# A new order of work behind the last depthwise convolution: scores, values and keys moved among TensorE, VectorE and ScalarE

## The reference, cut to what matters

```python
q, k, v = proj(Wq, bq), proj(Wk, bk), proj(Wv, bv)      # of X, per image (256, 32)
scores = jnp.einsum('bic,bjc->bij', q, k)
a = jax.nn.softmax(scores, axis=1)                      # over i
x = jnp.einsum('bij,bjc->bic', a, v)
return X + x
```

## Time and profile before

| | us |
|---|---|
| median of 3 runs | 115.43 |
| the three runs | 114.87 to 115.98 |
| the profiled execution | 114.63 |
| its span | 112.8 |

### The profile page before, as it was taken

One profiled execution on the slowest core, in us unless ns is written; L12 is line 12 of the kernel. 1 busy time (PEld: TensorE's weight loads), 2 busy tenths in 40 slices (PEclk: granted clock), 3 DMA queues, 4 the chain that ended last, 5 costly groups with the idle time before them and its releaser, 6 DMA issues.

```text
span 112.8 us, 5243 instructions
## 1 busy us (share of the span) xinstructions
PE 95.6 (85%) x2376; PEld 53.0 (47%) x2376; DVE 76.1 (67%) x154; ACT 86.7 (77%) x204; POOL 12.6 (11%) x25
## 2 busy tenths in 40 slices
PE   0193999989978999989987999989799999997660
PEld 0021477665525468324543663345454665575320
DVE  0004996534739897999578889936473889889751
ACT  4049787597998738896579899757989989879950
POOL 7010000000000000000000003893000040004200
PEclk9999589999999999999999999999999999999999
DMA  2890098870000000000000000000000100020022
GB/s 54 254 360 33 5 103 131 93 112 6 0 6 9 0 9 6 0 6 6 0 6 0 6 6 0 0 6 0 6 6 0 68 31 0 6 85 11 0 93 93
DMA packets 2261, 4.55 MB, mean 40 GB/s; under 512 B 576, under 2 KB 832, under 8 KB 2240
## 3 DMA queue, kind: packets, MB, share of 16 engines
q1 hardware_dynamic: 2096, 4.20, 16.1%
q10 hardware_dynamic: 144, 0.03, 0.2%
HBM read 1.96 MB, written 1.05 MB: 27 GB/s over the span
## 4 chain that ended last, share of the span: by engine, by line
PE 54%; ACT 19%; DVE 11%; DMA 7%; SPq 4%; issue 3%; ACTq 0%; DVEq 0%
PE ps L399 13%; ACT prob L771 7%; PE ps L482 6%; ACT hpad L722 5%; DMA x<-x_in 5%; PE ps L447 4%; PE ps L510 4%; DVE unit L936 4%; PE ps L494 3%; PE ps L475 3%; ACT prob L758 3%; DMA prob<-npad 3%; PE ps L287 3%; PE ps L383 3%; PE ps L298 2%
## 5 line engine op out<-in xcount | busy, mean ns | idle before, releaser
L399 PE MATMUL ps<-hpad,third 32*32 32x450 f32 (+2 forms) x864 | 36.5, 563 | 0.6 <-ACT hpad L722 0.4
L771 ACT ACTIVATE prob<-ps,smax 128x256 f32<-128x256 f32 x56 | 25.8, 479 | 3.7 <-DVE smax L983 3.6
L936 DVE SCALAR_TENSOR_TENSOR unit<-hpad,third,unit 128x544 f32<-128x544 f32 x32 | 23.9, 797 | 0.0
L983 DVE TENSOR_REDUCE smax<-ps 128x2 f32<-128x512 f32 x26 | 16.6, 685 | 6.5 <-PE ps L494 3.4
L399 PEld LDWEIGHTS ps<-hpad,third 32*32 32x32 f32 x864 | 14.0, 103 | 8.9 <-issue 4.2
L264 POOL TENSOR_TENSOR v_tok<-v_tok,row_inv 128x256 f32<-128x256 f32 x7 | 5.1, 740 | 88.8 <-DVE row_inv L993 88.8
L771 ACT ACTIVATION_READ_ACCUMULATOR prob<-ps,smax 128x1 f32 x56 | 11.8, 210 | 0.0
L722 ACT ACTIVATE hpad<-ps,third 128x1024 f32<-128x1024 f32 x8 | 8.7, 1115 | 2.9 <-PE ps L383 2.4
L863 DVE SCALAR_TENSOR_TENSOR npad<-x,first,rstd 128x256 f32<-128x256 f32 x8 | 3.5, 480 | 10.1 <-ACT rstd L700 10.1
L510 PE MATMUL ps<-prob,v_tok 128*32 128x256 f32 x128 | 8.1, 382 | 2.3 <-ACT prob L758 1.1
L691 ACT ACTIVATE swapped<-ps 128x512 f32<-128x512 f32 x8 | 4.5, 594 | 7.2 <-PE ps L287 7.2
(11 more groups left out here) (87 smaller groups left out, 144.7 us busy)
## 6 DMA issues: line engine op xcount, KB each, us to landing
prob<-npad SPq DMA_DIRECT2D x16, 74.4 KB, 2.9
x<-x_in SPq DMA_DIRECT2D x4, 256.0 KB, 5.6
y<-m SPq DMA_DIRECT2D x3, 256.0 KB, 2.6
third<-third_in SPq DMA_DIRECT2D x1, 456.5 KB, 6.7
second<-second_in SPq DMA_DIRECT2D x1, 401.5 KB, 5.8
y<-m SPq DMA_DIRECT2D x2, 128.0 KB, 1.9
first<-first_in ACTq DMA_DIRECT2D x1, 33.0 KB, 4.3
```

What stands on the lines that cost most here:

```text
L399: last = pe.matmul(inside(pixels(ps[quadrant(rotated(r, g)), banks[g], :]), tap), c3("taps")[quadrant(r), tap * C:(tap + 1) * C], inside(p ...
L771: last = act.activation(prob[:, G * (slot_turn(s) % PROBS) + g, jt * NPIX:(jt + 1) * NPIX], ps[:, banks[q], jt * NPIX:(jt + 1) * NPIX], AC ...
L936: dve.scalar_tensor_tensor(out=sums, in0=source, scalar=weight, in1=sums, op0=ALU.mult, op1=ALU.add).then_inc(unit_step, 1)
L983: dve.tensor_reduce(smax[:, s, 2 * q:2 * q + 2], ps[:, banks[q], :].rearrange("p (j i) -> p j i", j=2), AX_X, ALU.max, negate=True).then_i ...
```

## The change

On TensorE, behind `fc2_units(0, 6)`:

- the order was weighted values 2, last tap, key and query of slot 0, weighted values 3, V of chunk 2, scores 0, key and query of slot 1, V of chunk 0, the second linear layer of chunk 3. It becomes V of chunk 2 (into bank 7), last tap, key and query of slot 0, weighted values 2 (into bank 0, behind `conv_gelu` 9), scores 0, key and query of slot 1, weighted values 3 (into bank 1), the second linear layer.
- the scores of slot 1's quadrants 2 and 3 go ahead of the keys and queries of slots 6 and 7; V of chunk 0 (into bank 2) comes behind these.
- `weighted_values(5, ...)` moves between the two halves of slot 6's scores. The second half waits for `y_ready` 2 and `v_ready` 3 in place of `y_ready` 4; `y_ready` 4 is now waited for ahead of slot 7's scores.

On ScalarE the key of slot 1 is gone, and the exponentials of slot 1 are split after two quadrants instead of after one. On VectorE the key of slot 1 is added (`key_and_query(1, 2)`), `maxima(1, (0,))` goes ahead of `finish_block_slot(7, 0)`, `finish(3, 1)` comes between the maxima of slot 1, and the rest follows TensorE's new order.

```diff
             pe.wait_ge(exp_done, 14)
-            weighted_values(2, 7)
+            values(2, 7)
             conv_taps(3, 8, 9, LOW)
             pe.wait_ge(exp_done, 15)
             query_and_key(0, 4)
+            pe.wait_ge(conv_gelu, 9)
+            weighted_values(2, 0)
             pe.wait_ge(exp_done, 16)
-            weighted_values(3, 5)
-            pe.wait_ge(conv_gelu, 9)
-            values(2, 0)
-            pe.wait_ge(y_ready, 2)
+            pe.wait_ge(v_ready, 2)
             pe.wait_ge(q_ready, 5)
             pe.wait_ge(k_by_vector, 1)
             scores(0, range(G), HIGH)
             pe.wait_ge(conv_gelu, 11)
             query_and_key(1, 2)
-            values(0, 1)
+            weighted_values(3, 1)
             pe.wait_ge(conv_gelu, 12)
-            pe.wait_ge(v_ready, 2)
+            pe.wait_ge(y_ready, 1)
             fc2_hidden_slots(3, (3, 0))
             fc2_conv_slots(3, (3, 0))
             pe.wait_ge(q_ready, 6)
-            pe.wait_ge(k_ready, 5)
+            pe.wait_ge(k_by_vector, 2)
             for q in range(2):
                 pe.wait_ge(exp_done, 17 + q)
                 scores(1, (q,), HIGH)
+            pe.wait_ge(exp_done, 20)
+            scores(1, (2, 3), HIGH)
             query_and_key(6, 3)
             query_and_key(7, 0)
-            pe.wait_ge(exp_done, 20)
-            scores(1, (2, 3), HIGH)
-            weighted_values(4, 1)
-            weighted_values(5, 2)
+            values(0, 2)
+            pe.wait_ge(exp_done, 21)
+            weighted_values(4, 4)
             pe.wait_ge(q_ready, 8)
-            pe.wait_ge(k_ready, 7)
+            pe.wait_ge(k_ready, 6)
             scores(6, (0, 3), LOW)
+            pe.wait_ge(exp_done, 22)
+            weighted_values(5, 5)
+            pe.wait_ge(y_ready, 2)
+            pe.wait_ge(v_ready, 3)
+            scores(6, (1, 2), LOW)
             pe.wait_ge(y_ready, 4)
-            scores(6, (1, 2), LOW)
             pe.wait_ge(exp_done, 24)
             scores(7, range(G), HIGH)
@@ ScalarE
             act.preload_act_table_set(exp_tables)
-            key_slot(1, 2)
             pixel_exp(0, HIGH)
-            pixel_exp(1, HIGH, (0,))
+            pixel_exp(1, HIGH, (0, 1))
             key_slot(6, 3)
             act.wait_ge(q_ready, 7)
             key_slot(7, 0)
-            pixel_exp(1, HIGH, (1, 2, 3), 1)
+            pixel_exp(1, HIGH, (2, 3), 2)
             pixel_exp(6, LOW, (0, 3, 1, 2))
@@ VectorE
             finish_block(0, 6)
+            values(2, 7)
             key_and_query(0, 4)
-            finish(2, 7)
-            finish(3, 5)
-            values(2, 0)
             invert_sums(4)
             invert_sums(5)
+            finish(2, 0)
             maxima(0, (0, 1), HIGH, 7)
-            dve.wait_ge(k_ready, 5)
-            query(1, 2)
-            values(0, 1)
+            key_and_query(1, 2)
             maxima(0, (2, 3), HIGH, 7)
             finish_block_slot(6, 3)
+            maxima(1, (0,), HIGH, 8)
             finish_block_slot(7, 0)
-            maxima(1, (0,), HIGH, 8)
             maxima(1, (1,), HIGH, 9)
+            finish(3, 1)
+            maxima(1, (2,), HIGH, 10)
             dve.wait_ge(qk_of_slot, slot_of_qk(7))
             query(7, 0)
-            dve.wait_ge(k_ready, 6)
+            maxima(1, (3,), HIGH, 10)
+            dve.wait_ge(k_ready, 5)
             query(6, 3)
-            maxima(1, (2, 3), HIGH, 10)
-            finish(4, 1)
-            finish(5, 2)
+            values(0, 2)
+            finish(4, 4)
             maxima(6, (0, 3), LOW, 11)
+            finish(5, 5)
             maxima_of_two(6, 1, LOW, 12)
```

## The result

The changed kernel took 115.6 us (median of 20 runs, 115.24 to 117.16) beside 115.81 us for the kernel before (20 runs, 114.51 to 119.57). The ratio of after to before is 1.0058, with a 95% interval from 1.0032 to 1.0084. So the change made the kernel slower by about 0.6%, some 0.7 us; the medians point the other way because six of the 20 executions before and one of the 20 after were slow ones (over 1.5% above the fastest of their kernel), which the ratio leaves out. The profiled execution took 115.24 us with a span of 113.5 us (114.63 and 112.8 before). The forecast was +0.73 us (+0.6%), 113.5 us in span, 115.4 us for the profiled execution and 116.1 us for the median. The sum and the span were met; the 116.1 us stood 0.5 us above the 115.6 measured.

The account below looks back on a forecast made before the run. TensorE's list was taken to bound the kernel up to slot 6's scores, then ScalarE's exponentials; slot 7's start moving from 104.97 to 105.70 gave +0.73 us, added to the 115.43 median: 116.1 us, range 115.0 to 117.0.

Parts of the forecast that it names:

- The sum: Start of slot 7's exponentials on ScalarE, and the end with it, moves from 104.97 to 105.70: +0.73 us.
- The hole: TensorE waits 0.85 us ahead of weighted values 2 until bank 0 is free at 88.15.
- ScalarE's gaps of 1.0 and 0.75: ScalarE waits a full microsecond ahead of slot 1's exponentials and 0.75 us in the middle of slot 6's.
- The key's move: With slot 1's key on VectorE, ScalarE starts slot 0's exponentials at 91.20 instead of 91.91.
- no difference: Rival: slot 6's second-half wait is hidden by overlap or a shorter ScalarE gap; 0 to +0.3 us, 115.4 to 115.7; chance 0.18.
- The drain: Changing tiling mode drains TensorE between slot 6's scores and weighted values 5; without it the sum would be +0.2.
- lateness of 0.3 for X of slot 7: On TensorE, slot 7's key and query end about 0.3 us behind slot 6's, since X comes at 96.35.
- waits by semaphore cost 0.05 to 0.35: Unknown cost of waits, 0.05 to 0.35 us; the first activation behind the table load stood 0.35.
- Both paths meet at 99.40 to 99.45: VectorE's query 6 and TensorE's weighted values 4 both allow slot 6's first scores at 99.40 to 99.45.
- Second half of slot 6. Here is the loss: Weighted values 5 between slot 6's score halves delay the second to 101.48; ScalarE waits 0.75 us.
- The slow one: Rival: late X of slot 7 puts its projection behind slot 6's on TensorE; +1.5 us, 116.9; chance 0.20.
- faster: Rival: ScalarE's early start of 0.71 is kept and its gaps close; about -1.2, 114.2; chance 0.04 in full, 0.06 in part.

Follow-up runs that it names:

- key_back: Changed kernel with slot 1's key back on ScalarE, ahead of slot 0's exponentials; stretch (L440 to last output tile's start) 27.85 us, ratio to before 1.0099.
- w5_behind: Changed kernel with weighted values 5 behind both halves of slot 6's scores; stretch 27.18 us, ratio to before 1.0086.
- fill: hole_and_filler with weighted values 5 moved behind slot 6's scores; stretch 26.41 us, ratio to before 0.9977.
- hole_and_filler: no_hole with keys and queries of slots 6 and 7 back between the halves of slot 1's scores; stretch 26.86 us, ratio to before 1.0016.
- w5_ahead: Changed kernel with weighted values 5 ahead of both halves of slot 6's scores; stretch 27.71 us, ratio to before 1.0159.
- no_hole: Changed kernel with weighted values 2 (bank 7) and 3 (bank 0) both ahead of slot 0's scores, filling TensorE's hole; stretch 27.48 us, ratio to before 1.0161.

## Why the prediction was right, and where it wasn't

**Steps that held.** On the changed kernel's own clock, 0.16 us ahead of before: weighted values 2 at 88.04 (88.18 forecast, 88.02 on that clock), scores of slot 0 at 89.04 (89.18), exponentials of slot 0 at 91.04 (91.20), first half of slot 6's scores at 99.23 (99.40), slot 7's exponentials at 105.61 (105.70). The hole is 0.68 us by the profile, which counts from the end of the last matmul before it, where the forecast's 0.85 counted from when the next could have started (0.76 by the rows: 86.09 plus the 1.19 that key and query of slot 0 take in the earlier trace rows, to 88.04); its end is right. ScalarE's gaps of 1.0 and 0.75 were 0.90 and 0.68. The key's move gave the early start that it was priced at, 0.71, and key_back shows 0.40 of that at the end. The sum, +0.73 us, was +0.76 in the stretch. That it agrees to 0.03 us is in part luck: keys and queries of slots 6 and 7 started 0.08 later than forecast on the common clock (96.00 for 95.92) and took 0.13 less (1.14 for 1.27).

**The time itself.** The 116.1 us came from adding the sum to a median of three runs (115.43), which stood 0.8 us above the profiled execution. The other figure of the forecast, 115.4 for the profiled execution, was measured at 115.24. By its time alone, 115.6 us, the result would belong to the rival "no difference" (115.4 to 115.7), and the stated range was wide; it is the ratio and the stretch that show the forecast's +0.7.

**The drain.** Two quadrants of slot 6's scores (32x128 tiles) at 99.23 keep weighted values 5 (128x32) away until 100.29, 1.06 us for half a slot. The forecast's sum with the drain was +0.7, without it +0.2. No run takes the drain away; w5_behind takes the group from between the halves, which is worth 0.27 of that difference of 0.5, and fill against hole_and_filler 0.45. The Trainium skill, TensorEngine Tiling (Array Packing), section Key Properties, says that a change of tiling mode drains TensorE; the trace agrees by the 1.06 us. It doesn't single the drain out: the 128x32 tiles of weighted values also cover the rows on which the two quadrants' scores run, and that alone might hold them back; no run separates the two.

**Terms that were mis-sized.** Keys and queries of slots 6 and 7 were given 1.0 and a lateness of 0.3 for X of slot 7. They took 1.14 (96.00 to 97.14; 1.05 in the earlier trace rows), because X of slot 7 was written 0.08 behind their start (95.61 + 0.47 on VectorE) and not 0.27. The lateness itself is passed on one for one, as the forecast had it: in hole_and_filler X of slot 7 is written 0.23 behind the start of the projections, and they take 1.28 (94.41 to 95.69). Weighted values ahead of the second linear layer, priced at 1.00, took 0.89 (91.11 to 92.00). V of chunk 2 in place of weighted values 2, priced at +0.09, moved the last tap by 0.22 (2.08 us behind L440, 1.86 before), and the hole took it up. And "waits by semaphore cost 0.05 to 0.35" misread a row: in the 0.35 us ahead of slot 1's key ScalarE waited for TensorE's group itself, which ends at 91.47 (90.40 + 1.07), 0.06 ahead of ScalarE's start.

**What the forecast had wrong in its mechanism.** "Both paths meet at 99.40 to 99.45" left open whether VectorE or TensorE holds slot 6's first half. VectorE was busy without idle time from 95.00 to 99.9, as forecast, but query 6 was written at 98.99 and TensorE came at 99.23: TensorE's list held it.

```profile
98.52 0.47 DVE L956 TENSOR_SCALAR rstd<-ps,third 128x256 f32<-128x256 f32 x1
```

And "Second half of slot 6. Here is the loss" gave the whole cost to one place. w5_ahead shows that putting weighted values 5 back gains nothing. What the runs support instead is an account in three parts, each the difference of two stretches: from before to fill -0.28 (the rest of the new order, with weighted values 5 behind), then +0.45 for putting weighted values 5 between the halves, then +0.59 for opening the hole and taking the filler away, together +0.76. The forecast met the sum because its timeline carried all three; it named only one, and it priced the hole without asking what filling it would release.

**The rivals.** The slow one needed X of slot 7 to push its projection behind slot 6's; 1.14 instead of 2.0 excludes it. No difference (up to +0.3 us, 1.0026) and faster are excluded by the interval from 1.0032 to 1.0084, the first of them narrowly. The reason for faster, ScalarE's early start, was real (0.87 us earlier on the raw clock, 0.71 on the common one) and lost in the next gap.

**Not settled.** What in the rest of the new order makes fill 0.28 faster than before isn't taken apart: weighted values 5 behind slot 6's scores in the kernel before, the one edit that might give it alone, was not run. The three parts of the account are differences in this sequence of edits; in another (w5_behind first, 0.27) they come out otherwise. They rest on one profile each, and for w5_behind, w5_ahead and no_hole the ratios lie above what the stretches give. And w5_ahead's 0.2 us on VectorE are read from its trace, not tested.

## What to carry to other kernels

An engine that starts earlier is worth only what the next hand-over lets through: write the hand-over times down one after the other until the last engine, as the three gaps here show. Where two holds cover each other, undoing either gives nothing (0.03 more and 0.11 less here) and undoing both gives 0.59, so a null result for one edit doesn't clear it. In a queue whose order is fixed, ask of every group ahead of the critical one whether anybody needs it yet: after V of chunk 0 (97.14 to 98.22) six microseconds passed before its weighted values (104.71), and moving one group of 1.09 us was worth 0.76.

## What the runs showed of the hardware

Two groups on TensorE cost 0.11 us more where the next one uses another tile shape. Weighted values take 0.89 us start to start ahead of the second linear layer (both 128x32 tiles) and 1.00 ahead of scores (32x128), in one and the same kernel; the second linear layer of chunk 0 takes 0.89 ahead of weighted values in before (83.38 to 84.27) and 1.00 ahead of V (128x128) after (83.22 to 84.22).

A group that waits in the middle still overlaps with its first half where both use separate tiles. Keys and queries of slots 6 and 7 take 1.05 us together without a wait, 1.14 with slot 7's X 0.08 us late and 1.28 with it 0.23 us late.

From one execution to the next the part behind L440 repeats to 0.01 us (25.65 twice), while the start of L440 differed by 0.58 us between the same two profiles (83.85 and 83.27) and by up to 5.2 us over all thirteen, the more the later and the deeper the granted clock fell in the first 30 us. The ratios over whole executions had intervals 0.4 to 1.1% wide; the stretch gave the differences that they couldn't.
